# Activation loads and stores, piece loads and twelve weight parts issued by SP, and a maximum over partitions on GpSimd

## The reference

```python
def _L0_attn_ref(hidden_states, Wq, bq, Wk, bk, Wv, bv, Wo, bo):
    q = apply_rope(apply_rope(split_heads(h @ Wq.T + bq), freqs_abs), freqs_temp)
    k = apply_rope(apply_rope(split_heads(h @ Wk.T + bk), freqs_abs), freqs_temp)
    v = split_heads(h @ Wv.T + bv)
    scores = where(causal, q @ k.T / sqrt(16), -inf)
    return merge_heads(softmax(scores) @ v) @ Wo.T + bo

def _L0_ffn_ref(x, gate_w, up_w, down_w, gate_s, up_s, down_s):
    hdn = silu((x @ gate_w.T) * gate_s) * ((x @ up_w.T) * up_s)
    return (hdn @ down_w.T) * down_s

x = x + layernorm(attn(layernorm(x)))
x = x + layernorm(ffn(layernorm(x)))
```

## Time and profile before

| | us |
|---|---|
| median of three runs | 2676.25 |
| lowest, highest | 2672.62, 2683.75 |
| the profiled execution | 2674.29 |
| its span, first to last instruction | 2672.6 |
| PE busy in it | 2449.1 |
| mean granted clock of TensorE | 0.979 of full speed |

### The profile page before, as it was taken

The page is one execution under the profiler, slowest core; times in us unless marked ns, Lnnn a source line. Parts: engine busy times, 40 slices in busy tenths (PEclk is TensorE's granted clock), DMA queues, the critical chain, the costliest instruction groups (busy, mean ns, idle before and its releaser), DMA issues.

```text
span 2672.6 us, 54196 instructions
## 1 busy us (share of the span) xinstructions
PE 2449.1 (92%) x18816; PEld 1124.0 (42%) x18816; DVE 1954.3 (73%) x5956; ACT 1439.3 (54%) x1918; POOL 1174.8 (44%) x1521
## 2 busy tenths in 40 slices
PE   3889998998989999999999996799999999999997
PEld 1334434443434434434434432344444444444443
DVE  5789888898888899998999885355545555555554
ACT  3577776776777777777777765332222222222221
POOL 3566766766767767767767764210000000000000
PEclk8899999999999999999999998899999999999999
DMA  4344555555555555555555545311111111211111
GB/s 166 111 131 146 174 152 166 170 159 165 168 150 164 171 165 185 181 171 183 180 176 182 157 142 221 116 45 66 47 47 50 60 47 47 77 48 47 47 47 47
DMA packets 193249, 332.45 MB, mean 124 GB/s; under 512 B 34048, under 2 KB 123776, under 8 KB 179840
## 3 DMA queue, kind: packets, MB, share of 16 engines
q1 hardware_dynamic: 172384, 249.38, 29.9%
q10 hardware_dynamic: 20640, 80.23, 8.6%
HBM read 200.82 MB, written 127.67 MB: 123 GB/s over the span
## 4 chain that ended last, share of the span: by engine, by line
PE 53%; DVE 14%; issue 11%; POOL 11%; ACT 6%; DMA 3%; SPq 1%; POOLq 0%; ACTq 0%; DVEq 0%
PE banks L1435 11%; PE banks L1437 11%; DVE banks L1006 7%; PE banks L1323 6%; PE banks L1449 5%; PE banks L1453 5%; PE banks L1281 3%; PE banks L1283 3%; PE banks L1282 3%; PE banks L1295 2%; ACT probs L739 2%; POOL probs L602 2%; POOL shared L583 2%; POOL shared L581 2%; PE banks L1309 2%
## 5 line engine op out<-in xcount | busy, mean ns | idle before, releaser
L1006 DVE CUSTOM_DVE_ANT_0 banks<-banks,causal 128x512 f32<-128x512 f32 (+3 forms) x2048 | 941.4, 517 | 64.4 <-PE banks L1295 64.1
L739 ACT ACTIVATE probs<-banks,exp_scale 128x1024 f32<-128x1024 f32 x640 | 710.5, 1110 | 166.9 <-PE banks L1309 165.7
L1435 PE MATMUL banks<-probs,shared 128*128 128x512 f16 x1408 | 533.8, 379 | 2.6 <-DVE probs L1204 1.8
L1437 PE MATMUL banks<-probs,shared 128*128 128x512 f16 x1408 | 533.6, 379 | 0.0
L863 ACT ACTIVATE kT<-banks,gate_scale 128x512 f32<-128x512 f32 x176 | 120.9, 687 | 645.3 <-PE banks L1437 645.3
L1213 DVE SCALAR_TENSOR_TENSOR kT<-banks,up_scale,kT 128x512 f32<-128x512 f32 x176 | 131.8, 749 | 410.7 <-PE banks L1437 410.7
L1281 PE MATMUL banks<-shared 128*128 128x128 f16 (+1 forms) x1536 | 383.3, 279 | 43.2 <-issue 16.3
L664 POOL TENSOR_TENSOR f_rstd<-f_var,neg_half 128x4 f32<-128x4 f32 x32 | 32.2, 1007 | 879.9 <-DVE f_var L1189 636.9
L1282 PE MATMUL banks<-shared 128*128 128x128 f16 (+1 forms) x1536 | 379.5, 277 | 0.0
L1283 PE MATMUL banks<-shared 128*128 128x128 f16 (+1 forms) x1536 | 379.2, 277 | 0.0
L602 POOL TENSOR_SCALAR_AFFINE_SELECT probs<-probs 128x512 f32<-128x512 f32 x512 | 355.4, 717 | 32.9 <-ACT probs L739 32.4
(11 more groups left out here) (123 smaller groups left out, 3521.6 us busy)
## 6 DMA issues: line engine op xcount, KB each, us to landing
slots<-shared SPq DMA_DIRECT2D x260, 128.0 KB, 9.8
qT<-slots SPq DMA_DIRECT2D x128, 256.0 KB, 3.7
kT<-slots SPq DMA_DIRECT2D x128, 256.0 KB, 4.0
weighed<-oT SPq DMA_DIRECT2D x128, 256.0 KB, 5.0
probs<-x SPq DMA_DIRECT2D x32, 1024.0 KB, 4.7
slots<-shared SPq DMA_DIRECT2D x256, 64.0 KB
spread<-recips SPq DMA_DIRECT2D x64, 256.0 KB
averaged<-weighed SPq DMA_DIRECT2D x64, 256.0 KB
```

The costliest lines, as they stand in the source:

```text
L739: nc.scalar.activation(probs[:, g % 2, u, :, :], ts[:, :, :], ACT.Exp, scale=exp_scale[:, 0:1]).then_inc(ts_read, 1)
L1006: last = nc.vector.tensor_tensor_reduce(out=scores, in0=scores, in1=causal[:, T - P * (qt + 1):T], scale=1.0, scalar=-3e38, op0=ALU.add, o ...
L1435: nc.tensor.matmul(gu[:, bank, :], hi[:, c, cols], f_xT_hi[:, c, :], start=c == 0, stop=False)
L1437: last = nc.tensor.matmul(gu[:, bank, :], hi[:, c, cols], f_xT_lo[:, c, :], start=False, stop=end and not with_rest)
```

## The change

The loads of x into `xn`, the stores of x1 and the loads of `xr` move from ScalarE's body to SP's, and stand there at the end of step 9, 14 (was 15) and 19 (was 24). The loads of pieces move to SP as well and keep their steps. The second pass of pieces waits for `f_largest_reduced`. The feed-forward weights come in twelve parts of 704 KB, from s = 18 to s = 38 of body 15. ScalarE keeps the stores of split pieces and four small transfers. In the opening the way through `tops` is gone: GpSimd reduces `largest` over the partitions, and its body -1 begins behind that.

```diff
@@ -388,6 +386,7 @@
+        WEIGHTS_AT = (18, 19, 21, 23, 24, 26, 28, 29, 31, 33, 36, 38)
         PIECE_LOAD, PIECE_MAX, PIECE_HI, PIECE_LO, PIECE_OUT, PIECE_REST = 4, 8, 9, 13, 14, 18
@@ -417,11 +416,6 @@
-            sp.wait_ge(largest_ready, 1)
-            sp.dma_start(tops, largest[:, 0:4]).then_inc(largest_out, 16)
-            sp.wait_ge(largest_out, 16)
-            sp.dma_start(spread[:, :], tops.rearrange("(o p) n -> o (p n)", o=1).broadcast_to([P, 4 * P])).then_inc(largest_in, 16)
-
             def send_slots(i, n):
@@ -454,6 +448,26 @@
                                  shift_rows[4 * pair:4 * pair + 4, g % 2, :]).then_inc(shift_in, 16)
+
+            def load_piece(m):
+                n, k = divmod(m % NP, NP // 3)
+                if m < NP:
+                    wait_if_any(sp, piece_max, m)
+                else:
+                    sp.wait_ge(f_largest_reduced, 1)
+                    wait_if_any(sp, piece_lo, m - NP)
+                sp.dma_start(raw_piece[:, :], raws[n][:, PIECE * k:PIECE * (k + 1)]).then_inc(piece_in, 16)
+
+            def load_ffn_weights(m):
+                n, k = divmod(m, 4)
+                if m == 0:
+                    sp.wait_ge(piece_out, 16 * NP)
+                    sp.wait_ge(v_full, NC * NB)
+                    sp.wait_ge(qk_lo, 8 * NB)
+                    sp.wait_ge(slots_out, 64 * 8 * NB)
+                quarter = slice(k * 2 * PIECE, (k + 1) * 2 * PIECE)
+                sp.dma_start(part(2 * n * G, 2 * G).bitcast(F16).rearrange("p (h e) -> p h e", h=2)[:, :, quarter],
+                              halves[n, :, :, quarter]).then_inc(f_weights_in, 16)
@@ -508,6 +522,21 @@
                             fetch_weighed(i + of, c)
+                    if s == 9 and exists(i + 2):
+                        sp.wait_ge(xT_full, NC * (i + 2))
+                        sp.dma_start(xn[:, :, :], x[i + 2, :, :, :]).then_inc(x_in, 16)
+                    if s == 14 and exists(i - 2):
+                        sp.wait_ge(x1_ready, NT * (i - 1))
+                        sp.dma_start(x1[i - 2, :, :, :], xr[:, :, :]).then_inc(x1_out, 16)
+                    if s == 19 and exists(i - 2) and exists(i - 1):
+                        sp.wait_ge(x1_out, 16 * (i - 1))
+                        sp.dma_start(xr[:, :, :], x[i - 1, :, :, :]).then_inc(xr_in, 16)
+                    for first_body, pass_at in ((FIRST_PASS, 0), (SECOND_PASS, NP)):
+                        m = piece_at(i, s, PIECE_LOAD, first_body)
+                        if m is not None:
+                            load_piece(pass_at + m)
+                    if i == NB - 1 and s in WEIGHTS_AT:
+                        load_ffn_weights(WEIGHTS_AT.index(s))
@@ -659,11 +688,13 @@
                                               minus_mean[:, :], offset[:, :], offset_ready)
+            pool.wait_ge(largest_ready, 1)
+            nc.gpsimd.partition_all_reduce(largest_all[:, :], largest[:, 0:4], P, RMAX).then_inc(largest_reduced, 1)
             def ffn_root(i, ready, v, out, done):
-            body(-1, (offset_ready, 1))
+            body(-1, (largest_reduced, 1))
             body(0, (roped_done, 6))
@@ -784,25 +815,12 @@
                             normalise_projected(i - 2, t)
-                    if s == 9 and exists(i + 2):
-                        act.wait_ge(xT_full, NC * (i + 2))
-                        act.dma_start(xn[:, :, :], x[i + 2, :, :, :]).then_inc(x_in, 16)
-                    if s == 15 and exists(i - 2):
-                        act.wait_ge(x1_ready, NT * (i - 1))
-                        act.dma_start(x1[i - 2, :, :, :], xr[:, :, :]).then_inc(x1_out, 16)
-                    if s == 24 and exists(i - 2) and exists(i - 1):
-                        act.wait_ge(x1_out, 16 * (i - 1))
-                        act.dma_start(xr[:, :, :], x[i - 1, :, :, :]).then_inc(xr_in, 16)
                     m = piece_at(i, s, PIECE_HI, SECOND_PASS)
...
                         store_piece(m)
-                    for first_body, pass_at in ((FIRST_PASS, 0), (SECOND_PASS, NP)):
-                        m = piece_at(i, s, PIECE_LOAD, first_body)
-                        if m is not None:
-                            load_piece(pass_at + m)
                     if i == SCALES_IN and s == 14:
@@ -817,31 +835,11 @@
                             [P, 3 * P])).then_inc(rest_in, 16)
-                    if i == NB - 1 and s in (19, 21, 24):
-                        load_ffn_weights((19, 21, 24).index(s))
-
-            def load_piece(m):
-                n, k = divmod(m % NP, NP // 3)
-                if m < NP:
-                    wait_if_any(act, piece_max, m)
-                else:
-                    act.wait_ge(piece_max, NP)
-                    wait_if_any(act, piece_lo, m - NP)
-                act.dma_start(raw_piece[:, :], raws[n][:, PIECE * k:PIECE * (k + 1)]).then_inc(piece_in, 16)
...
                 act.dma_start(halves[n, :, :, PIECE * k:PIECE * (k + 1)], split_piece[:, :, :]).then_inc(piece_out, 16)
-
-            def load_ffn_weights(n):
-                if n == 0:
-                    act.wait_ge(piece_out, 16 * NP)
-                    act.wait_ge(v_full, NC * NB)
-                    act.wait_ge(qk_lo, 8 * NB)
-                    act.wait_ge(slots_out, 64 * 8 * NB)
-                act.dma_start(part(2 * n * G, 2 * G).bitcast(F16).rearrange("p (h e) -> p h e", h=2),
-                              halves[n]).then_inc(f_weights_in, 16)
@@ -924,9 +922,6 @@
                                         ALU.max).then_inc(largest_ready, 1)
-                dve.wait_ge(largest_in, 16)
-                nc.vector.tensor_reduce(largest_all[:, :], spread[:, :].rearrange("p (q n) -> p n q", n=4), AX.X,
-                                        ALU.max).then_inc(largest_reduced, 1)
                 power_of_two_scales(dve, nc, setup, largest_all[:, :], power[:, :], scale[:, :],
@@ -1477,7 +1472,7 @@
             pe.wait_ge(f_setup_done, 2)
-            pe.wait_ge(f_weights_in, 48)
+            pe.wait_ge(f_weights_in, 16 * len(WEIGHTS_AT))
...
```

More of the change, by code:

```diff
@@ L71, in sandwich @@
 def sandwich(nc, x, wT, bias_row, bias_columns, rope_cos, rope_sin, gateT, upT, downT, gate_s, up_s, down_s, slots, weighed,
-             recips, tops, f_tops, f_rests, halves, x1, out):
+             recips, f_tops, f_rests, halves, x1, out):
     ctx = ExitStack()
@@ L251, in sandwich @@
         largest_ready = sem("largest_ready")
-        largest_out = sem("largest_out")
-        largest_in = sem("largest_in")
         largest_reduced = sem("largest_reduced")
@@ L1551 @@
     recips = nc.dram_tensor("recips", (NC, P, 8 * T // P), F32, kind="Internal").ap()
-    tops = nc.dram_tensor("tops", (P, 4), F32, kind="Internal").ap()
     f_tops = nc.dram_tensor("f_tops", (P, 5), F32, kind="Internal").ap()
@@ L1557 @@
              ap["gateT"], ap["upT"], ap["downT"], ap["gate_s"], ap["up_s"], ap["down_s"], slots, weighed,
-             recips, tops, f_tops, f_rests, halves, x1, out)
+             recips, f_tops, f_rests, halves, x1, out)
     r = run_bass_kernel_spmd(nc, [arrays], core_ids=[0])
```

## The result

The changed kernel takes 2641.74 us as the median of four runs (2640.44 to 2645.96); the kernel before, on the same chip, 2674.43. The ratio is 0.9868, with a 95% interval of 0.9842 to 0.9894: 32.7 us faster, where 32 were forecast. The profiled execution took 2640.44 us (span 2638.7), 33.9 less than the 2674.29 before. Two executions further down that took 9498.65 and 4875.39 us, far outside all others, count in no median, ratio or trace.

A forecast was written before the change was run, and what follows sets the result against it. PE, busy 92% of 2672.6 us, was taken to bound the kernel, with its waits to be won; -4.0 (opening) - 26 + 6 (bodies 0 to 14) - 8 (body 15) = -32 us gave 2644.3 us, range 2622 to 2674.

The forecast's parts named there:

- Opening, -4.0: Start of kernel: one GpSimd reduction replaces the way through memory, -4.0 us, with ends of -7.0 and 0.
- 3.2 - 7.2: Opening: GpSimd's reduction taken at 3.2 us, replacing 7.2 us of store, load and DVE reduction on the path.
- The -26: Bodies 0 to 14: 37.0 us of oT copy waits for its store vanish, 0.7 of them reaching the end.
- more than forecast: Rival: averaging loads also lose their neighbours, 20 of 193.4 us of waits reach the end, 2624 us; chance 0.13.
- nothing that is waited for: Bodies 0 to 14: some 90 issues removed from ScalarE cost it nothing waited for, taken as 0.
- The +6: Bodies 0 to 14: at step 14, 1376 KB on SP delay slot stores and shift rows, +6 us, between 0 and 9.8.
- Step 19 is better off: 1024 KB, with the next stores two steps away as well: Bodies 0 to 14: xr's load on SP at step 19 delays later transfers less than step 14's 1376 KB.
- the slower rival: SP's one queue holds small transfers back, shift rows late in bodies 0 to 14 and body 15: 2696 us; chance 0.12.
- The waits move, they don't go: Rival: xr at step 19 meets step 21's slot stores and step 23's averaging loads instead: 2670 us; chance 0.22.
- Body 15, -8: Last attention body: twelve weight parts remove PE gaps of 3.12 and 5.01 us, -8 us, ends of -14 and +2.
- The end, 0: Feed-forward part: left alone by the change; the last two weight parts have some 25 us for 4 us of transfer.
- Even bodies: Attention bodies in the profile after: all even at 95 to 99 us.

The follow-up runs named there:

- the second trace: The changed kernel run once more, unchanged, alongside the follow-up experiments: 2640.42 us, ratio 0.9879 to the kernel before.

## Why the prediction was right, and where only its total was

By runs, the 33 us are made of the reduction, -7.3; everything in SP's queue at the old steps, with the weights in twelve parts, -42.2 (2665.69 to 2623.53); and the new steps, +17 (2623.53 to 2640.42). That the sum came out within 1 us was luck. Bodies 0 to 14 won 6 us less than forecast and the end lost 3, body 15 won 9 more and the opening 2.

*Opening, -4.0: right in mechanism, mis-sized.* The term "3.2 - 7.2" took 3.2 us for the reduction, by GpSimd's longest instruction of the opening. It measured 0.39 us, near the lower bound of 0.20, and PE gained 6.7 us. The choice between the two ends went by what the instruction does, where its 128x4 elements would have been the better guide here. That the library load is hidden by the 11 us before `largest` was right; bare it would have cost 7.9 us. The Trainium skill, "GPSIMD Engine Reference", section "Instruction dispatch", has about 6 us for the first call of freshly loaded code. Here the trace shows 7.88.

*Bodies 0 to 14, -26 + 6: two errors that cancelled.* The -26 held that all the oT waits vanish, and that 0.7 of the 37.0 us in these bodies reach the end. At the change's steps the waits fell by only 32 of 45.8 us (25 in the second trace), and what is left stands mostly behind xr's new place. With xr at step 24 on SP's queue 5.2 us are left, so the mechanism was right. But moving the queue gains 33 us in these bodies at the old steps, more than 26. Averaging's waits are 148.5 us there, from 193.4. I had that as the rival "more than forecast" and left it out of the sum; how much of the 33 each kind of wait gives no run separates. The Trainium skill's rule that several issuers save issue time only ("DMA: Bandwidth & Descriptors", "Issuing engines are not separate DMA queues") would have given 0. The 1491.9 and 1458.5 us for the same transfers at the same steps speak against it, with at most 4.5 us of issue time in them. They agree with the turns between rows that the prediction took, though no run shows the turns themselves.

The issues were put at 0, "nothing that is waited for", by one of them that ran beside an exponential. The waits view of before has 5.0 us of ScalarE standing behind issues in 10 places, so the term was not quite nothing, and at the new steps it grows to 14.0 us when ScalarE makes them.

The +6 was put on the wrong transfer. The step that failed is "Step 19 is better off: 1024 KB, with the next stores two steps away as well". I computed the drain of step 14 down to the shift rows and judged step 19 by its size alone. Step 14's store costs nothing (x1 back at 15: no difference). Step 19's load costs 17 us, because SP itself waits for the slot stores behind it, and the averaging load and the oT store of step 24 stand behind SP's wait. So the slower rival, "SP's one queue holds small transfers back", was real in kind. Its indicator, waits of PE for the shift rows over 20 us, stayed quiet at 2.3 us, since the victims were others. Two slips of working changed nothing: at the slow rate the 384 KB of slots take 3.1 us and not 1.8, which makes the shift rows 6 us late and not 5; and five parts of the weights stand at steps 18 to 24, not six.

"The waits move, they don't go" named this very place, the slot stores of step 21 and the averaging loads of step 23. Its price was wrong in one way: it took all of the 26 as lost where about half was.

*Body 15, -8: right for the gaps, without the clock.* The idle time fell by 8.7 us, about the 8 that I took. The clock, which I had left for the range, gave 8.0 more in this pair of traces (0.84 to 0.92), of which 4.5 may be scatter. The total of 16.7 lies beyond the forecast's end of -14. No gap over 3 us was to be left, and the longest is 2.11 (3.45 in the second trace); the lowest clock in 20 us is 0.83. With three loads on SP body 15 took 95.9 us, so what moved to SP's queue gives 6.5 to 10 us by itself (from 102.4 or 106.3) and splitting 6 more. With the twelve parts on ScalarE it is as short, 89.0, so once they are split their queue gives nothing more.

*The end, 0: wrong by +2.8.* I checked that the last parts arrive in time for the first gate product, 25 us away, and not what is loaded at the same time. It is the x load of the feed-forward, wanted at once. The parts delay it from the other queue too (7.2 us for 7.7, and 5.0 without them), so here it is mostly the traffic beside it and not the place in the queue.

*Even bodies: not so.* The bodies were to be even at 95 to 99 us. Bodies 2 to 6 are (96.2 to 98.1); 7 to 13 are not (99.5 to 102.4), and with xr at 24 bodies 8, 10 and 13 still take 101 us. What keeps these longer than the first six was not settled.

## What to carry to other kernels

In this kernel a 1 MB transfer cost 17 us or nothing by what stood behind it in its own queue and by what the issuing engine next waited for. So follow each transfer that the engine issues after it up to the engine's next wait on a landing, and then what is queued behind that wait. One number, step 24 in place of 19, was worth as much as half of the whole change. To test whether a queue matters, change the issuer and nothing else, at the steps of the kernel that you compare with: at other steps ScalarE's own issues came into it as well. When a sum of terms comes out right, take the terms apart by single edits all the same; the two that cancel hide the next gain.

## What the hardware showed that was not expected

The maximum over 128 partitions of four columns took 0.39 us on GpSimd, and the code that it needs 7.88 us to load, in an idle time with no instruction in it. Moving 48 loads of 352 KB back to the other queue cost 14 us. An issue on ScalarE took 0.35 us where it stood first and 1.5 us where another stood just ahead of it, and ScalarE was idle for 2.2 us behind three of them. And two executions of one kernel differed by up to 5 us in a single body while their sum over fifteen bodies differed by 2.
